# A two-layer decoder on one core: how split query and key rows pass through memory to be stacked, and where GpSimd adds two output biases

## Chip, cores and metric

The kernel runs on one core of a Trainium2 chip. The metric is the device time of one execution, in microseconds. The engines are named as in the profile: PE (TensorE), PEld (its weight loads), DVE (VectorE), ACT (ScalarE), POOL (GpSimd) and SP (SyncE, which here only issues DMAs).

## The reference, cut to what matters

Six sublayers over x of 8 sequences (b) of 256 rows and 256 columns, each followed by a layer norm. The change lies in the fourth (D) and fifth (E).

```python
def _L1_attn_ref(x, Wqkv, bqkv, Wout, bout, proj):      # stage D
    ...
    q, k, v = jnp.split(x @ Wqkv.T + bqkv, 3, axis=-1)  # 16 heads of 16, relu(q proj), relu(k proj), causal, chunks of 128
    ...
    return out @ Wout.T + bout
def _L1_xattn_ref(query, key_value, Wq, bq, Wk, bk, Wv, bv, Wo, bo):   # stage E
    ...
    q = (query @ Wq + bq).reshape(B, Nq, H, D).transpose(0, 2, 1, 3)
    k = (key_value @ Wk + bk).reshape(B, Nkv, H, D).transpose(0, 2, 1, 3)
    v = (key_value @ Wv + bv).reshape(B, Nkv, H, D).transpose(0, 2, 1, 3)
    attn = jnp.clip(jnp.einsum('bhqd,bhkd->bhqk', q, k) * scale, -CLAMP, CLAMP)
    attn = jax.nn.softmax(attn, axis=-1)
    ...
    x = jnp.einsum('bhqk,bhkd->bqhd', attn, v).reshape(B, Nq, Cq)
    return x @ Wo + bo
...
x = _layernorm(x + _L0_attn_ref(x, ...))        # A
x = _layernorm(x + _L0_xattn_ref(x, ctx_768, ...))   # B
x = _layernorm(x + _L0_ffn_ref(x, ...))         # C
x = _layernorm(x + _L1_attn_ref(x, ...))        # D
x = _layernorm(x + _L1_xattn_ref(x, ctx_768, ...))   # E
x = _layernorm(x + _L1_ffn_ref(x, ...))         # F, two of eight experts a token
```

In E a score is a product of a query and a key row of 16 numbers. The kernel keeps near fp32 accuracy with pairs: hi is the rounded value, lo is the rest.

## The kernel before

The stages A, B and C are done first. D and E run together as a software pipeline over the 8 sequences; then come F (experts, in blocks of tokens) and the last norm. The order inside D and E is written out by `de_steps` (L104): each item has a round in which it starts, a priority, and rounds for its steps. `in_rounds` sorts them, and every engine walks through the same list `DE` and does its own part of each step. Sequence b's E scores (`PAIR`, eight steps of two head pairs) start 18 rounds behind its D steps, so that they stand between D's steps of b+2.

What the change touches:

- `EPRE` steps 1 and 2 make keys and queries of E. PE multiplies, ACT writes `qk_hi` and `qk_raw` (L1362, L1365), POOL subtracts for `qk_lo` (L620). There is one `qk_hi` and one `qk_lo`: ACT and POOL wait until the tensor before (keys, then queries, `n = 2 * b + which`) is in memory (`w_qk`, L1360 and L619).
- `stack_heads` (L779) is SP's part. It stores hi and lo (128 rows each, L786) to the DRAM tensor `split_qk`, waits until both have landed (L787), and loads them back with their rows reordered: 8 loads of 16 partitions by 8 KB for each tensor (L795). Keys go into `k_e` (named `xt_lo` in the profile, since they lie in its room), queries into `q_e` (`xt_hi`). The matmul of scores (L1090) then contracts over 64 partitions that hold r = 0..3, one side stacked as hi, lo, hi, lo and the other as hi, hi, lo, lo. It waits for all 16 loads of b (L1084).
- SP issues the DMAs one by one. Its queue also carries the context load (L801) and the store of x rows (L806).
- `finish` on POOL (L583) adds the output bias to x in its step 0 (L592: two adds of 128x256 for b), for D in `DFIN` step 0 and for E in `EFIN` step 0, and takes the layer norm's power in step 1. The bias waits until PE has transposed the old x (`old.filled`, L589). DVE's `resid` (L1682) waits for it through `s_xb` (L1679).
- `EFIN` step 7 issues four indirect DMAs on POOL that scatter 128 codes of 4 bytes each into `slot_codes` (L640). `EFIN` step 7 of b-1 and step 0 of b share a round in the list, and step 7 stands first.

```python
load(held[part], f(src[:, :, :]).rearrange("p c s -> p (c s)"), w_qk)          # L786, once for hi, once for lo
...
heads = held[r // 2 if which else r % 2].rearrange("(i d j) s -> i d (j s)", i=2, d=DH)
...
load(f((q_e if which else k_e)[b % 2][rows, :, :]).rearrange("p j s -> p (j s)"), heads[i], l_qk[b % 2])   # L795
```

## Time and profile before

| what | value |
|---|---|
| three runs | 1616.68, 1610.22, 1615.24 us; median 1615.24 |
| the profiled execution's own time, and its span | 1623.73 us; 1621.9 us |
| mean granted TensorE clock in it | 0.904 |
| PE, PEld, DVE, ACT, POOL busy, share of the span | 83, 70, 68, 35, 50% |
| stretch 780 to 1210 us (most of D and E): PE, DVE, ACT, POOL busy | 338.8, 285.0, 164.1, 145.8 of 430 us |
| stretch 1210 to 1290 us (end of E, routing): the same | 38.4, 38.3, 16.4, 33.3 of 80 us |
| chain that ended last: share of DMA, of SP's queue | 10%, 2% |

Read it so: busy shares are averages over stages with different limits; for a change in D and E, what counts is the stretch from about 760 to 1290 us, and in it the waits of the engine that the others follow. A row of a timeline gives start, busy time, engine, line, operation, tiles and count, and in brackets how long the engine stood idle before it and who ended that.

### The profile page before, as it was taken

How to read it: one execution, taken by the hardware profiler on the slowest of the kernel's cores; microseconds unless marked ns; L12 is line 12 of the kernel's file. 1: busy time of each engine (PE TensorE's matmuls, PEld its weight loads, DVE VectorE, ACT ScalarE, POOL GpSimd, SP SyncE). 2: the span in 40 equal slices, each digit the busy share in tenths (PEclk: the TensorE clock that was granted, in tenths of full speed). 3: DMA queues.
4: the chain of work that ended last, by engine and by line, in shares of the span. 5: the costliest groups of instructions: out<-in, count | busy, mean ns of one | idle time of the engine just before them, and what ended most of it. 6: DMA issues, size and time to landing. Idle time of an engine off the chain costs nothing.

```text
span 1621.9 us, 23438 instructions
## 1 busy us (share of the span) xinstructions
PE 1347.4 (83%) x9047; PEld 1137.9 (70%) x9047; DVE 1109.1 (68%) x1877; ACT 561.0 (35%) x1138; POOL 816.9 (50%) x762
## 2 busy tenths in 40 slices
PE   5787799989989989978788989788656199999990
PEld 5776678868868878865566656556544199999990
DVE  5889776676576676634476767567654388888886
ACT  2355311111021121113244434334322166666662
POOL 3333556656566656640123334244335378888852
PEclk9896799999999999989899999899776599999995
DMA  5100233323223322210444155153340366666624
GB/s 164 30 16 11 69 92 91 104 85 92 77 91 91 104 78 79 84 59 7 78 83 78 38 67 71 26 84 57 59 59 7 110 239 230 219 212 236 219 72 156
DMA packets 53534, 154.99 MB, mean 96 GB/s; under 512 B 10822, under 2 KB 25641, under 8 KB 45488
## 3 DMA queue, kind: packets, MB, share of 16 engines
q1 hardware_dynamic: 41248, 91.87, 24.0%
q0 software_dynamic: 12176, 61.63, 10.8%
q8 instruction: 72, 1.18, 0.3%
q14 instruction: 38, 0.31, 0.1%
HBM read 136.60 MB, written 18.70 MB: 96 GB/s over the span
## 4 chain that ended last, share of the span: by engine, by line
PE 54%; DVE 19%; DMA 10%; issue 6%; ACT 5%; POOL 4%; SPq 2%; ACTq 0%; DVEq 0%; POOLq 0%
PE bank L385 12%; PE bank L387 12%; PE bank L386 12%; PE bank L1193 8%; DMA xt_hi<-split_qk 5%; PE bank L393 4%; DMA split_qk<-qk_lo 3%; PE bank L1035 2%; DVE hid_hi L1598 2%; SPq L706 2%; DVE topE L1723 2%; DVE hf L1614 1%; DVE shiftE L1732 1%; PE bank L1111 1%; PE bank L1022 1%
## 5 line engine op out<-in xcount | busy, mean ns | idle before, releaser
L512 POOL TENSOR_TENSOR wpiece_lo<-wraw,wpiece_hi 128x1024 fp32r<-128x1024 f32 x88 | 216.8, 2463 | 7.4
L1600 DVE TENSOR_TENSOR hid_lo<-hf,hid_hi 128x512 fp32r<-128x512 f32 x96 | 215.8, 2248 | 3.3
L385 PE MATMUL bank<-hid_hi,wpiece_lo 128*128 128x512 f32 x512 | 204.1, 399 | 13.3 <-DVE hid_lo L1600 13.3
L387 PE MATMUL bank<-hid_hi,wpiece_hi 128*128 128x512 f32 x512 | 202.6, 396 | 0.0
L386 PE MATMUL bank<-hid_lo,wpiece_hi 128*128 128x512 f32 x512 | 202.3, 395 | 0.0
L510 POOL TENSOR_SCALAR wpiece_hi<-wraw 128x1024 fp32r<-128x1024 f32 x88 | 95.6, 1086 | 192.6 <-PE bank L387 188.7
L1598 DVE CAST hid_hi<-hf 128x512 fp32r<-128x512 f32 x96 | 76.9, 801 | 131.1 <-ACT hf L1292 130.0
L626 POOL TENSOR_SCALAR staging<-staging 128x1024 f32<-128x1024 f32 x64 | 66.6, 1041 | 176.4 <-ACT staging L1377 176.3
L1292 ACT ACTIVATE hf<-bank,ffn_scales 128x512 f32<-128x512 f32 x64 | 44.1, 690 | 299.1 <-PE bank L387 299.1
L385 PEld LDWEIGHTS bank<-hid_hi,wpiece_lo 128*128 128x128 f32 x512 | 98.1, 192 | 39.2 <-DVE hid_lo L1600 19.0
L1723 DVE TENSOR_REDUCE topE<-bank 128x4 f32<-128x1024 f32 x64 | 77.9, 1218 | 65.8 <-PE bank L1090 65.7
L1377 ACT ACTIVATE staging<-bank 128x512 f32<-128x512 f32 x128 | 70.2, 596 | 151.3 <-PE bank L1111 86.4
L387 PEld LDWEIGHTS bank<-hid_hi,wpiece_hi 128*128 128x128 f32 x512 | 97.8, 191 | 20.8
L386 PEld LDWEIGHTS bank<-hid_lo,wpiece_hi 128*128 128x128 f32 x512 | 98.2, 192 | 20.3
L1193 PE MATMUL bank<-w_hi,gh_lo 128*128 128x256 f32 x368 | 105.8, 288 | 5.6 <-issue 2.6
L1434 ACT ACTIVATE gf<-bank,w1raw 128x256 f32<-128x256 f32 x184 | 77.2, 471 | 91.4 <-PE bank L387 91.4
L385 PE MATMUL bank<-xgT_hi,w_lo 128*128 128x256 f32 x368 | 106.7, 290 | 1.4 <-DVE xgT_lo L1850 1.4
L386 PE MATMUL bank<-xgT_lo,w_hi 128*128 128x256 f32 x368 | 104.6, 284 | 0.0
L387 PE MATMUL bank<-xgT_hi,w_hi 128*128 128x256 f32 x368 | 104.6, 284 | 0.0
L1193 PE MATMUL bank<-w_hi,gh_hi 128*128 128x256 f32 x368 | 104.1, 283 | 0.0
L1193 PE MATMUL bank<-w_lo,gh_hi 128*128 128x256 f32 x368 | 104.1, 283 | 0.0
L670 POOL TENSOR_TENSOR w_lo<-w2raw,w_hi 128x256 fp32r<-128x256 f32 x92 | 91.7, 1023 | 11.4 <-ACT w_hi L1409 10.9
(353 smaller groups left out, 3805.0 us busy)
## 6 DMA issues: line engine op xcount, KB each, us to landing
wraw<-in_C_w SPq DMA_DIRECT2D x88, 512.0 KB, 3.6
xt_lo<-split_qk SPq DMA_DIRECT2D x64, 128.0 KB, 5.2
xt_hi<-split_qk SPq DMA_DIRECT2D x64, 128.0 KB, 6.2
split_qk<-qk_hi SPq DMA_DIRECT2D x16, 256.0 KB, 4.4
split_qk<-qk_lo SPq DMA_DIRECT2D x16, 256.0 KB, 3.8
yc<-y_rows SPq DMA_DIRECT2D x16, 256.0 KB, 5.8
ctx_raw<-in_ctxT SPq DMA_DIRECT2D x16, 192.0 KB, 3.6
xraw<-in_xT SPq DMA_DIRECT2D x8, 256.0 KB, 3.8
```

What stands on the lines that cost most here:

```text
L385: pe.e.matmul(o, sl, mh, start=start and i == 0, stop=False)
L386: pe.e.matmul(o, sh, ml, start=False, stop=False)
L387: made = pe.e.matmul(o, sh, mh, start=False, stop=stop and i == n - 1)
L510: pool.mark(pool.e.tensor_scalar(pair[0], raw, 1.0, 0.0, ALU.mult, ALU.add))
L512: pool.e.tensor_tensor(pair[1], raw, f(pair[0]), ALU.subtract).then_inc(done, 1)
L670: pool.e.tensor_tensor(w2[n % 6][1][:, 1, :], w2_cols(*divmod(n, NQ))[:, 1, :], f(w2[n % 6][0][:, 1, :]), ALU.subtract).then_inc(s_w2lp, 1)
L1193: made = pe.e.matmul(u.ap[:, t * D:(t + 1) * D], hh[:, i, st], ww[:, i, :], start=fc == 0 and k == 0 and t == 0, stop=fc == FC - 1 and k == 2,
L1377: act.e.activation(prob_e[n % 3][:, i, :, :], u.ap[:, :].rearrange("p (k s) -> p k s", k=TT), ACT.Exp, scale=scale_e).then_inc(u.drained, 1)
L1434: made = act.e.activation(gf[n % 2][:, i * BT:(i + 1) * BT], u.ap[:, i * BT:(i + 1) * BT], ACT.Gelu, bias=w1raw[j % 4][:, c:c + 1])
L1598: dve.mark(dve.e.tensor_copy(hi[:, o, :], hf[o % 2][:, :]))
L1600: dve.e.tensor_tensor(lo[:, o, :], hf[o % 2][:, :], f(hi[:, o, :]), ALU.subtract).then_inc(s_hid, 1)
L1723: dve.mark(dve.e.tensor_reduce(top[:, :], scores, AX.X, ALU.max))
```

## The change

The stores now put the rows where they will be read. `split_qk` is laid out as two tensors of [2 (i), 4 (r), 64 rows, 512]. Of hi and of lo each, SP issues four stores of 64 partitions by 2 KB (i = 0, 1 for two values of r), so each value is written twice. One load of 128 partitions by 8 KB then brings a tensor back. `w_qk` becomes one semaphore for keys and one for queries. POOL adds D's bias in step `XT` (behind the transposes of C's x) and E's bias in `DFIN` step 3 (behind the transposes of D's x).

```diff
@@ -241,7 +241,7 @@
 
         x_rows = nc.dram_tensor("x_rows", (B * S, D), F32, kind="Internal").ap()
         y_rows = nc.dram_tensor("y_rows", (TOPK * B * S, D), F32, kind="Internal").ap()
-        split_qk = ring(2, lambda i: nc.dram_tensor(f"split_qk{i}", (2, 2, P, KC * S), F32, kind="Internal").ap())
+        split_qk = ring(2, lambda i: nc.dram_tensor(f"split_qk{i}", (2, 2, 4, 4 * DH, KC * S), F32, kind="Internal").ap())
         slot_codes = nc.dram_tensor("slot_codes", (NE * B * S + BT, 1), U32, kind="Internal").ap()
 
         def xt(b):
@@ -345,7 +345,7 @@
         s_dwo, s_ew = sem("dwo"), sem("ew")
         s_xb, s_cthi = {k: sem(f"xb_{k}") for k in "DE"}, {k: sem(f"ct_hi_{k}") for k in "DE"}
         s_vone, s_prob = sem("ones"), sem("e_prob")
-        s_qkhi, s_qklo, w_qk, l_qk = sem("e_qkhi"), sem("e_qklo"), sem("w_qk"), ring(2, lambda i: sem(f"l_qk{i}"))
+        s_qkhi, s_qklo, w_qk, l_qk = sem("e_qkhi"), sem("e_qklo"), ring(2, lambda i: sem(f"w_qk{i}")), ring(2, lambda i: sem(f"l_qk{i}"))
         s_rm, s_re, s_rf, s_rb, s_rs, s_sh = (sem(f"r_{n}") for n in ("m", "e", "f", "b", "s", "sh"))
         s_seen, s_slot = sem("r_seen"), sem("r_slot")
         w_rows, w_codes = ring(2, lambda i: sem(f"w_rows{i}")), ring(2, lambda i: sem(f"w_codes{i}"))
@@ -463,6 +463,11 @@
             u = use[stage, "x", b]
             line.wait_ge(u.drained, u.done)
 
+        def stored(line, n):
+
+            for which in range(2):
+                line.wait_ge(w_qk[which], 16 * 8 * ((n + 1 - which) // 2))
+
         def piece_done(m):
 
             s, n = divmod(m, NPIECE)
@@ -580,19 +585,17 @@
             for b in range(B - BPS, B):
                 ln_pow(pool, "C", b)
 
-            def finish(stage, step, b, bo, l_bo, n_bo):
-                if step == 0:
-                    before_it = "C" if stage == "D" else "D"
-                    old = use[before_it, "x", b]
-                    pool.wait_ge(l_bo, n_bo)
-                    pool.wait_ge(s_x[before_it], b + 1)
-                    pool.wait_ge(old.filled, old.full)
-                    for t in range(TT):
-                        x = x_tok[:, b * TT + t, :]
-                        made = pool.e.tensor_tensor(x, x, bo[:, :], ALU.add)
-                    made.then_inc(s_xb[stage], 1)
-                elif step == 1:
-                    ln_pow(pool, stage, b)
+            def add_bias(stage, b, bo, l_bo, n_bo):
+
+                before_it = "C" if stage == "D" else "D"
+                old = use[before_it, "x", b]
+                pool.wait_ge(l_bo, n_bo)
+                pool.wait_ge(s_x[before_it], b + 1)
+                pool.wait_ge(old.filled, old.full)
+                for t in range(TT):
+                    x = x_tok[:, b * TT + t, :]
+                    made = pool.e.tensor_tensor(x, x, bo[:, :], ALU.add)
+                made.then_inc(s_xb[stage], 1)
 
             last = use["C", "y", B - 1]
             pool.wait_ge(last.drained, last.done)
@@ -608,15 +611,19 @@
                     for i, n, pair, src in ((1, 48, eq, "E_wq"), (1, 64, ek, "E_wk"), (0, 80, ev, "E_wv"), (1, 80, eo, "E_wo")):
                         pool.wait_ge(l_stage[i], n)
                         split([w[:, :, :] for w in pair], staged(i, a[src]), s_ew)
-                elif name == "DFIN":
-                    finish("D", step, *args, dbo, l_db, 80)
+                elif name == "XT":
+                    add_bias("D", *args, dbo, l_db, 80)
+                elif name == "DFIN" and step == 1:
+                    ln_pow(pool, "D", *args)
+                elif name == "DFIN" and step == 3:
+                    add_bias("E", *args, ebo, l_eb, 64)
                 elif name == "EPRE" and step == 0:
                     context(B + args[0])
                 elif name == "EPRE" and step < 3:
                     b, = args
                     n, u = 2 * b + step - 1, use["E", "kq"[step - 1], b]
                     pool.wait_ge(u.drained, u.done)
-                    pool.wait_ge(w_qk, 32 * n)
+                    stored(pool, n)
                     pool.e.tensor_tensor(qk_lo[:, :, :], qk_raw[:, :, :], f(qk_hi[:, :, :]), ALU.subtract).then_inc(s_qklo, 1)
                 elif name == "PAIR" and step == 1:
                     b, p = args
@@ -626,8 +633,9 @@
                     pool.e.tensor_scalar(pr, pr, 1.0, 0.0, ALU.min, ALU.max).then_inc(s_prob, 1)
                 elif name == "EFIN":
                     b, = args
-                    finish("E", step, b, ebo, l_eb, 64)
-                    if step == 6 and b < B - 1:
+                    if step == 1:
+                        ln_pow(pool, "E", b)
+                    elif step == 6 and b < B - 1:
                         one_hot(pool, b)
                         set_shares(pool, b)
                     elif step == 7:
@@ -780,19 +788,19 @@
 
 
                 n, held = 2 * b + which, split_qk[b % 2][which]
-                sp.wait_ge(l_qk[b % 2], 16 * 16 * (b // 2))
+                sp.wait_ge(l_qk[b % 2], 16 * 2 * (b // 2))
                 for part, (src, done) in enumerate(((qk_hi, s_qkhi), (qk_lo, s_qklo))):
                     sp.wait_ge(done, n + 1)
-                    load(held[part], f(src[:, :, :]).rearrange("p c s -> p (c s)"), w_qk)
-                sp.wait_ge(w_qk, 32 * (n + 1))
+                    for r in range(4):
+                        if (r // 2 if which else r % 2) == part:
+                            for i in range(2):
+                                load(held[i, r], f(src[i * 4 * DH:(i + 1) * 4 * DH, :, :]).rearrange("p c s -> p (c s)"), w_qk[which])
+                sp.wait_ge(w_qk[which], 16 * 8 * (b + 1))
                 if b >= 2:
                     old = use["E", "s", b - 2, PAIRS - 1]
                     sp.wait_ge(old.filled, old.full)
-                for r in range(4):
-                    heads = held[r // 2 if which else r % 2].rearrange("(i d j) s -> i d (j s)", i=2, d=DH)
-                    for i in range(2):
-                        rows = slice((4 * i + r) * DH, (4 * i + r + 1) * DH)
-                        load(f((q_e if which else k_e)[b % 2][rows, :, :]).rearrange("p j s -> p (j s)"), heads[i], l_qk[b % 2])
+                load(f((q_e if which else k_e)[b % 2]).rearrange("p j s -> p (j s)"),
+                     held.rearrange("i r (d j) s -> (i r d) (j s)", j=4), l_qk[b % 2])
 
             for name, step, args in DE:
                 b = args[0]
@@ -1081,7 +1089,7 @@
                 elif name == "PAIR" and step == 0:
                     b, p = args
                     u = use["E", "s", b, p]
-                    pe.wait_ge(l_qk[b % 2], 16 * 16 * (b // 2 + 1))
+                    pe.wait_ge(l_qk[b % 2], 16 * 2 * (b // 2 + 1))
                     pe.wait_ge(u.drained, u.turn)
                     for t in range(TT):
                         for i in range(2):
@@ -1357,7 +1365,7 @@
                     act.wait_ge(l_eb, 64)
                     act.wait_ge(u.filled, u.full)
                     act.wait_ge(s_qklo, n)
-                    act.wait_ge(w_qk, 32 * n)
+                    stored(act, n)
                     for c in range(KC):
                         made = act.e.activation(qk_hi[:, c, :], u.ap[:, c * S:(c + 1) * S], ACT.Identity, bias=bias[:, c:c + 1])
                     made.then_inc(s_qkhi, 1)

```

**SP, keys and then queries of one sequence** (`xt_lo` are the keys stacked, `xt_hi` the queries). Before:

```order
L706 DMA split_qk<-qk_hi 128x512 [waits e_qkhi]
L706 DMA split_qk<-qk_lo 128x512 [waits e_qklo]
L706 DMA xt_lo<-split_qk 16x2048 [waits w_qk]
L706 DMA xt_lo<-split_qk 16x2048 x7
L706 DMA split_qk<-qk_hi 128x512 [waits e_qkhi]
L706 DMA split_qk<-qk_lo 128x512 [waits e_qklo]
L706 DMA xt_hi<-split_qk 16x2048 [waits w_qk]
L706 DMA xt_hi<-split_qk 16x2048 x7
```

Now, in the same place:

```order
L714 DMA split_qk<-qk_hi 64x512 [waits e_qkhi]
L714 DMA split_qk<-qk_hi 64x512 x3
L714 DMA split_qk<-qk_lo 64x512 [waits e_qklo]
L714 DMA split_qk<-qk_lo 64x512 x3
L714 DMA xt_lo<-split_qk 128x2048 [waits w_qk0]
L714 DMA split_qk<-qk_hi 64x512 [waits e_qkhi]
L714 DMA split_qk<-qk_hi 64x512 x3
L714 DMA split_qk<-qk_lo 64x512 [waits e_qklo]
L714 DMA split_qk<-qk_lo 64x512 x3
L714 DMA xt_hi<-split_qk 128x2048 [waits w_qk1]
```

Twenty DMAs a sequence become eighteen: the loads fall from 16 to 2, the stores rise from 4 to 16.

**POOL, in the middle of D and E, from one sequence's scatter on** (`ebo` is E's bias, `dbo` D's). Before:

```order
L640 DMA slot_codes<-codes,slot0 16640x1 [waits r_slot]
L640 DMA slot_codes<-codes,slot0 16640x1 x3
L592 TENSOR_TENSOR x_tok<-x_tok,ebo 128x256 [waits lnD_x]
L592 TENSOR_TENSOR x_tok<-x_tok,ebo 128x256
L626 TENSOR_SCALAR staging<-staging 128x1024 [waits drained4]
L419 TENSOR_TENSOR lnE_rstd1<-lnE_rstd1,minus_half 128x2 [waits lnE_var]
```

Now, the same place, and then the place ahead of the keys' lo part of the next sequence:

```order
L648 DMA slot_codes<-codes,slot0 16640x1 [waits r_slot]
L648 DMA slot_codes<-codes,slot0 16640x1 x3
L633 TENSOR_SCALAR staging<-staging 128x1024 [waits drained4]
L419 TENSOR_TENSOR lnE_rstd1<-lnE_rstd1,minus_half 128x2 [waits lnE_var]
```

```order
L597 TENSOR_TENSOR x_tok<-x_tok,dbo 128x256 [waits filled4,lnC_x]
L597 TENSOR_TENSOR x_tok<-x_tok,dbo 128x256
L633 TENSOR_SCALAR staging<-staging 128x1024 [waits drained6]
L597 TENSOR_TENSOR x_tok<-x_tok,ebo 128x256 [waits filled4,lnD_x]
L597 TENSOR_TENSOR x_tok<-x_tok,ebo 128x256
L627 TENSOR_TENSOR qk_lo<-qk_raw,qk_hi 128x512 [waits w_qk1,drained5]
```

E's bias no longer stands behind the four scatters of the sequence before it; both biases now stand ahead of a `qk_lo` of keys. PE, DVE and ACT keep their instructions in their order.

## Rows read from the trace of the kernel before

**Rows 1.** PE's waits, 700 to 1240 us: total us, times, longest

```profile
PE bank L1090 <- DMA xt_hi<-split_qk: 62.1, 7, 17.9
PE bank L1035 <- DVE shiftE L1732: 21.6, 17, 2.0
```

**Rows 2.** Timeline of PE: the first scores of b = 0, 1, 3, 4, 5, 6, 7

```profile
793.98 0.80 PE L1090 MATMUL bank<-xt_lo,xt_hi 64*128 64x256 f32 x4 [6.72 <-DMA xt_hi<-split_qk]
841.39 0.50 PE L1090 MATMUL bank<-xt_lo,xt_hi 64*128 64x256 f32 x4 [2.17 <-DMA xt_hi<-split_qk]
957.93 0.80 PE L1090 MATMUL bank<-xt_lo,xt_hi 64*128 64x256 f32 x4 [6.78 <-DMA xt_hi<-split_qk]
1023.40 0.80 PE L1090 MATMUL bank<-xt_lo,xt_hi 64*128 64x256 f32 x4 [9.98 <-DMA xt_hi<-split_qk]
1084.84 0.80 PE L1090 MATMUL bank<-xt_lo,xt_hi 64*128 64x256 f32 x4 [6.29 <-DMA xt_hi<-split_qk]
1146.18 0.80 PE L1090 MATMUL bank<-xt_lo,xt_hi 64*128 64x256 f32 x4 [12.24 <-DMA xt_hi<-split_qk]
1200.37 0.79 PE L1090 MATMUL bank<-xt_lo,xt_hi 64*128 64x256 f32 x4 [17.89 <-DMA xt_hi<-split_qk]
```

**Rows 3.** The chain: start, us until landed, lo stores (one of keys, seven of queries)

```profile
771.05 2.02 DMA split_qk<-qk_lo
777.18 6.96 DMA split_qk<-qk_lo
...
826.03 5.00 DMA split_qk<-qk_lo
...
935.28 5.34 DMA split_qk<-qk_lo
...
997.48 5.08 DMA split_qk<-qk_lo
...
1062.61 5.07 DMA split_qk<-qk_lo
...
1123.61 7.91 DMA split_qk<-qk_lo
...
1176.04 12.04 DMA split_qk<-qk_lo
```

**Rows 4.** The chain: the last of eight query loads, b = 0 and b = 4

```profile
787.29 6.64 DMA xt_hi<-split_qk
...
1005.71 17.64 DMA xt_hi<-split_qk
```

**Rows 5.** Timeline of POOL: the first scatter beside the loads of b = 4, 6, 7

```profile
1002.03 1.11 POOL L640 DMA_INDIRECT slot_codes<-codes,slot  x1 [0.17 <-issue]
...
1125.73 1.11 POOL L640 DMA_INDIRECT slot_codes<-codes,slot  x1 [0.54 <-DVE slot L1788]
...
1177.96 1.11 POOL L640 DMA_INDIRECT slot_codes<-codes,slot  x1 [0.41 <-DVE slot L1788]
```

**Rows 6.** Stretches: length, busy us of PE, PEld, DVE, ACT, POOL, then PEclk, DMA share, GB/s

```profile
993.00:1000.00 7.00, 7.00 (x64) 5.34 (x62) 4.48 (x16) 4.04 (x10) 3.11 (x8) 1.00 1.02 133
...
1006.00:1016.00 10.00, 7.42 (x66) 5.28 (x62) 7.18 (x17) 3.35 (x6) 5.15 (x6) 1.00 0.89 52
1285.50:1289.00 3.50, 0.40 (x2) 0.28 (x2) 1.16 (x6) 0.00 (x0) 1.56 (x2) 0.50 0.87 295
```

**Rows 7.** Timeline of PE, right behind the wait of b = 3

```profile
958.66 1.97 PE L393 MATMUL bank<-ident,shiftE 128*128 128x128 f32 x8
```

**Rows 8.** Timeline of DVE: `resid` of E for b = 6 and b = 7

```profile
1230.33 0.69 DVE L1682 TENSOR_TENSOR resid<-bank,x_tok 128x512 f32<-128x512 f32 x1 [3.50 <-POOL x_tok L592]
...
1256.84 0.69 DVE L1682 TENSOR_TENSOR resid<-bank,x_tok 128x512 f32<-128x512 f32 x1 [5.08 <-POOL x_tok L592]
```

**Rows 9.** Timeline of PE: the last product that the `resid` of b = 7 reads

```profile
1254.33 0.41 PE L387 MATMUL bank<-eo_hi,ctxT_E_hi 128*128 128x256 f32 x1
```

**Rows 10.** One line of DVE: ns min/median/max, first and last start

```profile
L1726 DVE SCALAR_TENSOR_TENSOR topE<-topE,lowE x64: 161/164/1253, 796.1 to 1233.5; 128x4 f32<-128x4 f32 x64
```

## The prediction, made before the changed kernel had run

> **What bounds the kernel now.** The page's chain of waits puts 10% of the span on DMAs, most of it on the stacked query and key rows. So I read next who waits for them: the waits of TensorE over stages D and E. PE stands idle 62.1 us for `xt_hi`, the last loads of the stacked queries, and the next wait there, for DVE's `shiftE`, is 21.6 us over 17 times [rows 1]. The timeline shows the 62.1 us one by one: 6.72, 2.17, 6.78, 9.98, 6.29, 12.24 and 17.89 us ahead of the first scores of b = 0, 1, 3, 4, 5, 6 and 7 [rows 2]; b = 2 does not wait. PE is the engine that the others follow there (338.8 of 430 us busy in the table), so those waits are on the path.
>
> Then the chain, for what a wait is made of. The lo part of the queries is ready and its store issued at 777.18, 826.03, 935.28, 997.48, 1062.61, 1123.61 and 1176.04 [rows 3]. From there to PE's first scores [rows 2] it takes 16.8, 15.4, 22.7, 25.9, 22.2, 22.6 and 24.3 us. For b = 4 that is 5.1 us for the store to land, 3.1 us until the last of eight loads is issued at 1005.71, and 17.6 us until it lands [rows 3, 4]. For b = 0 the last load lands in 6.6 us [rows 4]. The difference is the scatter: for b = 4 POOL's four scatters begin at 1002.03 [rows 5], and from 1006 to 1016 52 GB/s move where the keys' loads alone moved 133 GB/s at a full DMA share [rows 6]. A 128-row load of 8 KB rows (an expert's weights) runs at 295 GB/s [rows 6].
>
> **The change, part by part.**
>
> *The load.* 1 MB at 133 GB/s is 7.9 us, and b = 0 shows 3.1 + 6.6 = 9.7 us from the first issue to landing [rows 4]. At 295 GB/s it is 3.6 us, and landing adds about the 2.0 us that an unhindered store takes from issue to landing [rows 3]: 5.6 us. I take 5.6, since the row at 295 GB/s has the new load's shape; the upper bound is 9.7 (no gain).
> The Trainium skill (SBUF — State Buffer, "Door 1: The DMA port swizzle") says that 16 partitions reach 4 of 16 ports, 104 GB/s at 1 MiB, and 128 partitions 328 GB/s. The trace agrees in kind: 133 against 295 GB/s [rows 6].
>
> *The stores.* Hi and lo are now four stores each. SP issues at 0.46 us apiece (the last of eight loads starts 3.1 us behind the first), so the last lo store is issued 1.4 us behind the first and lands 2.0 us later [rows 3]: 3.4 us. Twice the bytes leave from 64 partitions; no row has that shape. Lower bound 3.4; upper bound, 512 KB at the 16-row rate of 133 GB/s behind as much of hi, about 8 us. I take 4.0, near the row of the unhindered store.
> By the same table of the skill, 64 partitions reach 8 ports and 196 GB/s, so 512 KB would take 2.7 us and a sequence's path would be about 1 us longer than my sum has it, some 6 us less gain in all; no row here shows it.
>
> *Path of a query, new.* 4.0 + 5.6 = 9.6 us from the ready lo part to the scores, where nothing else runs.
> - b = 0: ACT's queries wait for the keys' stores, which land about 2 us later than now, and the queries' stores meet the keys' load (1.5 us). 16.8 - 9.6 - 3.5 = 3.7 us saved of 6.7.
> - b = 1: 15.4 - 9.6 = 5.8, more than the 2.2 us waited. Saved 2.2.
> - b = 3, 4, 5: the scatters start some 4.6 us behind the lo store (997.48 and 1002.03 for b = 4 [rows 3, 5]), just as the load goes out. At 52 GB/s for 10 us [rows 6] they can cost a load anything from 0 to 11.0 us, the difference between b = 4 and b = 0 [rows 4]; I take 6, between the ends, since half of the new load is through before the queues are full. Saved: 22.7, 25.9, 22.2 less 9.6 less 6 = 7.1, 10.3, 6.6, each just over the 6.8, 10.0 and 6.3 waited. Saved 23.1.
> - b = 6, 7: the scatters start 2.1 and 1.9 us behind the lo store [rows 3, 5] and hit stores and load; I take 8. b = 7 also has its keys' stores late (2 us; its own lo store took 12.0 us [rows 3]). Saved 22.6 - 17.6 = 5.0 of 12.2 and 24.3 - 19.6 = 4.7 of 17.9.
>
> Sum: 38.7 us of 62.1.
>
> *The clock.* Behind a long wait the four score matmuls take 0.80 us, behind a short one 0.50 [rows 2], and the next eight transposes 1.97 us [rows 7]. Twice the time is the lower of the clock's two levels (a granted clock of 0.50, as in the third stretch of [rows 6], is 1.2 for 2.4 GHz), and PE had stood idle before it. Where a wait goes, I estimate 1 to 2 us saved behind it, bounds 0 and 2.5. Three waits go whole and others in part: 5 us.
>
> *E's bias.* For b = 6 `resid` waits 3.50 us for POOL, which issues four scatters first; PE and DVE are nearly empty there, and this stands on the path. For b = 7 the last product ends at 1254.74 [rows 9] and `resid` starts at 1256.84 [rows 8]: 2.1 of its 5.08 us of idleness. Moved, the adds come 18 rounds of the list early. Saved 5.6 us. Two more such waits, at b = 4 and 5, lie beside PE's waits for loads; they count for nothing alone, but would have come up next.
>
> *D's bias* moves along on an engine that is busy 146 of 430 us there; zero. Both biases now stand ahead of a keys' `qk_lo`. Their cover is POOL's idleness, and if it were gone the keys, not the queries, would be some 3 us later. SP's queue gets shorter (18 issues for 20), and the context load and the store of x rows behind it come earlier; zero.
>
> *What is late next.* With PE's pauses gone, the norm's chain and `shiftE` have less time beside them: 3 us lost, bounds 0 and 15 [rows 1].
>
> Together 38.7 + 5 + 5.6 - 3 = 46 us. The profiled execution took 1623.7 us, so it would become 1577.7. The median of the runs shown is 1615.2, 8.5 below it, so the median becomes **1569**.
>
> **The rivals.**
> 1. *The scatter holds the loads all the same.* The full 11.0 us come on top for b = 3 to 7. For: 52 GB/s whatever the ports [rows 6]. Against: one load has fewer pieces left when the scatters start. Saved: 3.7 + 2.2 for b = 0 and 1, 2.1, 5.3, 1.6, 2.0 and 1.7 for the rest, and the tail's 5.6: 24.2 us, 1591 us. Chance 0.17.
> 2. *All waits go.* 62.1, 7 of clock, 5.6: 75 us, 1540 us. It needs stores and load to overtake the scatters. Against: 12.0 us for one store of b = 7 [rows 3]. Chance 0.10.
> 3. *DVE and POOL collide.* The moved adds hold DVE: `L1726` takes 164 ns at the median and 1253 at most [rows 10], so one collision can cost 1.1 us. Sixteen pairs of adds in new places: 16 us, 1585 us. They could collide in their old places too, so the sign is open. Chance 0.05. The Trainium skill (SBUF — State Buffer, "Who interferes with whom") says that a DVE operation with two SBUF inputs waits for a whole GpSimd operation that reads SBUF, as `L1726` has.
> 4. *The waits move, nothing is won.* The chain of the norm and `shiftE` takes the place of the loads. Against: b = 2 has no wait for a load, and nothing long in its place. 1612 us, chance 0.04.
> 5. *Slower: the stores are the new wait.* Eight stores of 64 rows run at the 16-row rate: 1 MB a tensor is 7.9 us, for keys and again for queries, ahead of a load that stays at 9.7 us (the ports are not what limits it). Then each of seven paths grows by about 5 us: 35 us, less the tail's 5.6: 1645 us. It decides from where the stores cost more than the load gives back, a lo part that lands over 8 us after it is ready with a load at 9.7. Chance 0.04.
>
> **How the numbers follow.** The forecast has 0.60, the rivals 0.17, 0.10, 0.05, 0.04 and 0.04. The range is 1541 to 1595: below, all waits gone; above, the scatter in full, with 4 us for stores that land late. That leaves out rivals 4 and 5 and edges, under 2 in 10. 0.5% is 8 us, about what a measurement of this kernel can tell from no change. Faster by more: forecast and rivals 1 to 3, 0.92; within: rival 4, 0.04; slower: rival 5, 0.04.
>
> **What would show it.** In the changed profile: PE's wait for `xt_hi` near 23 us, almost all of it at b = 6 and 7; one query load landing in about 6 us at b = 0 to 2 and 6 to 16 us beside scatters; lo stores landing about 4 us after the first issue; no wait of `resid` for POOL; behind b = 4 no scores at 0.80 us. The prediction is wrong if b = 3 to 5 still wait over 3 us each (rival 1), if DVE or the norm's chain shows new waits of PE over 15 us in total (rival 4), or if a load of 128 rows takes over 8 us where no scatter runs.

## The result, and the profile after

The changed kernel takes 1573.1 us at the median (1571.1 to 1576.0) where the kernel before takes 1616.0 (1610.2 to 1624.4). The ratio is 0.973 with an interval of 0.969 to 0.978: faster. The prediction was 1569, its range 1541 to 1595.

The profiled execution of the changed kernel has a span of 1569.7 us and takes 1571.6, against 1621.9 and 1623.7 before: 52.1 us less. From the page of the changed kernel, busy time by engine, memory traffic, and the chain by engine:

```profile
PE 1332.3 (85%) x9047; PEld 1128.4 (72%) x9047; DVE 1114.2 (71%) x1877; ACT 559.8 (36%) x1138; POOL 816.0 (52%) x762
...
HBM read 136.60 MB, written 27.08 MB: 104 GB/s over the span
...
PE 58%; DVE 23%; issue 6%; ACT 5%; DMA 5%; SPq 2%; POOL 2%; ACTq 0%; DVEq 0%; POOLq 0%
```

DMAs are now 5% of the chain where they were 10%, although 8.4 MB more are written (27.1 for 18.7 MB).

To see where the 52.1 us went, cut both executions at the first product that makes a `feat` of D (`qkD` by `proj`) and at the start of the last scatter: stages A to C, then D and E. The windows of the changed kernel (length, busy us of PE, PEld, DVE, ACT, POOL, then PEclk, DMA share, GB/s):

```profile
0.00:711.20 711.20, 629.65 (x3182) 536.73 (x3182) 490.49 (x682) 162.71 (x310) 378.56 (x276) 0.94 0.27 80
711.20:1221.80 510.60, 418.95 (x3565) 312.66 (x3565) 348.73 (x685) 200.54 (x420) 189.82 (x246) 0.90 0.27 75
```

The same windows of the kernel before:

```profile
0.00:717.80 717.80, 636.75 (x3180) 542.55 (x3180) 489.32 (x682) 162.81 (x310) 381.38 (x278) 0.93 0.26 79
717.80:1274.60 556.80, 428.16 (x3565) 317.52 (x3565) 344.76 (x685) 201.78 (x420) 187.15 (x244) 0.86 0.34 54
```

D and E became 46.2 us shorter (556.8 to 510.6). In them PE is busy for 9.2 us less (428.2 to 419.0) with the same 3565 matmuls, at a mean granted clock of 0.90 for 0.86, and idle for 36.9 us less (128.6 to 91.7). Stages A to C, which the change doesn't touch, ran 6.6 us shorter in this execution, again nearly all of it PE's busy time (7.1 us). That part belongs to the execution, not to the change, and something of the kind can be in D and E too: two more profiles of the changed kernel, shown further on, have 516.1 and 518.5 us there, with PE busy for 424.5 and 423.8. The medians differ by 42.9 us.

PE's waits over stages D and E (700 to 1200 us, the total, the times and the longest), which answer to [rows 1]:

```profile
PE bank L1043 <- DVE shiftE L1740: 25.1, 22, 2.0
PE bank L1098 <- DMA xt_hi<-split_qk: 20.8, 3, 10.2
```

The wait for the query loads fell from 62.1 to 20.8 us, and the norm's `shiftE` is now the larger of the two, 3.5 us up (0.8 up in the second profile of this kernel). Which three waits are left, in the timeline of PE (as [rows 2]; the idle time stands in brackets):

```profile
782.65 0.51 PE L1098 MATMUL bank<-xt_lo,xt_hi 64*128 64x256 f32 x4 [1.63 <-DMA xt_hi<-split_qk]
1103.47 0.80 PE L1098 MATMUL bank<-xt_lo,xt_hi 64*128 64x256 f32 x4 [10.19 <-DMA xt_hi<-split_qk]
1153.61 0.80 PE L1098 MATMUL bank<-xt_lo,xt_hi 64*128 64x256 f32 x4 [8.99 <-DMA xt_hi<-split_qk]
```

These are b = 0, 6 and 7. Sequences 1 to 5 don't wait any more. The chain has the pieces of the same three (as [rows 3, 4]; start and us until landed, and of the four lo stores the last one's):

```profile
773.57 4.18 DMA split_qk<-qk_lo
777.76 4.84 DMA xt_hi<-split_qk
...
1087.46 8.28 DMA split_qk<-qk_lo
1095.75 7.67 DMA xt_hi<-split_qk
...
1137.43 8.34 DMA split_qk<-qk_lo
1145.79 7.78 DMA xt_hi<-split_qk
```

What is 4.2 and 4.8 us at b = 0 is 8.3 and 7.7 beside scatters. The order of events for b = 4 and b = 6 shows why one waits and the other doesn't. SP's timeline at b = 4, where four stores of lo precede one load:

```profile
976.70 2.54 SPq L714 DMA_DIRECT2D split_qk<-qk_lo  x4
981.50 0.33 SPq L714 DMA_DIRECT2D xt_hi<-split_qk  x1
```

and POOL's first scatter beside the loads of b = 3, 4 and 6 (each is followed by three more, 1.3 us apart):

```profile
925.57 1.24 POOL L648 DMA_INDIRECT slot_codes<-codes,slot  x1 [0.62 <-issue]
...
981.05 1.11 POOL L648 DMA_INDIRECT slot_codes<-codes,slot  x1 [0.17 <-issue]
...
1087.89 1.11 POOL L648 DMA_INDIRECT slot_codes<-codes,slot  x1 [0.17 <-issue]
```

For b = 4 the stores had landed and the load went out 0.45 us behind the start of the first scatter's issue; it still landed in 4.8 us. For b = 6 the scatters came 2.4 us behind the first lo store's issue, and neither the stores nor the load behind them landed in time:

```profile
1085.52 2.54 SPq L714 DMA_DIRECT2D split_qk<-qk_lo  x4
1095.75 0.33 SPq L714 DMA_DIRECT2D xt_hi<-split_qk  x1
```

Query loads take 4.8, 5.0, 4.9, 4.8, 4.8, 8.6, 7.7 and 7.8 us for b = 0 to 7. From the first lo store's issue to the load's issue it is 6.1, 4.9, 4.8, 4.4, 4.8, 4.8, 10.2 and 10.3 us. In the stretch of b = 0's load 305 GB/s move. The stretch of b = 6's stores, 1088 to 1098 us, has a mean of 58, but that is no steady rate (the last two lines):

```profile
778.50:782.60 4.10, 2.52 (x16) 1.39 (x14) 1.88 (x6) 1.02 (x1) 0.00 (x0) 1.00 0.84 305
1087.50:1089.90 2.40, 2.40 (x30) 1.86 (x29) 2.33 (x4) 1.39 (x3) 1.91 (x3) 1.00 0.84 285
1090.50:1095.70 5.20, 2.78 (x32) 1.69 (x28) 5.06 (x8) 1.36 (x3) 4.66 (x5) 1.00 0.02 1
```

The stores' bytes go at 285 GB/s and are through by about 1090. Then next to nothing moves for over 5 us, at a DMA share of 0.02, and the last store counts as landed only at 1095.74. What the scatters put off here is the landing, not the moving of bytes. The loads beside scatters look different. This is the load of b = 5, then that of b = 6:

```profile
1037.50:1043.20 5.70, 4.79 (x52) 4.04 (x50) 4.24 (x7) 0.38 (x1) 3.81 (x4) 1.00 0.86 53
1095.90:1100.50 4.60, 0.00 (x0) 0.00 (x0) 1.96 (x5) 1.09 (x2) 0.00 (x0) 0.71 0.72 50
```

For some 5 us they move 50 to 53 GB/s at a high DMA share, as in [rows 6], and then the rest at 273 and 349 GB/s (1043.2 to 1046 and 1100.5 to 1103.4 us). Why the one and why the other, the trace does not show.

DVE's `resid` of E, which waited 3.50 and 5.08 us for POOL [rows 8], now waits for PE's own product:

```profile
1181.16 0.69 DVE L1690 TENSOR_TENSOR resid<-bank,x_tok 128x512 f32<-128x512 f32 x1 [0.44 <-PE bank L387]
1204.00 0.69 DVE L1690 TENSOR_TENSOR resid<-bank,x_tok 128x512 f32<-128x512 f32 x1 [3.02 <-PE bank L387]
```

One wait is new, and the prediction had it for b = 0 and b = 7 alone: ACT, about to write the queries' `qk_hi`, stands for the keys' stores at all eight sequences. ACT's waits of the changed kernel:

```profile
ACT qk_hi L1370 <- DMA split_qk<-qk_lo: 34.1, 8, 5.3
```

It was 4.5 us over two times before.

### The profile page after: what moved, and what is told of

The parts are those of the page before. It is cut to its first block, busy times and chain, and to the rows that moved or that the text cites. A ratio compares the mean times of both kernels' runs of the same rounds, so it can differ in the third digit from the quotient of the medians.

```text
span 1569.7 us, 23427 instructions
## 1 busy us (share of the span) xinstructions
PE 1332.3 (85%) x9047; PEld 1128.4 (72%) x9047; DVE 1114.2 (71%) x1877; ACT 559.8 (36%) x1138; POOL 816.0 (52%) x762
## 3 DMA queue, kind: packets, MB, share of 16 engines
q1 hardware_dynamic: 45088, 100.26, 21.6%
## 4 chain that ended last, share of the span: by engine, by line
PE 58%; DVE 23%; issue 6%; ACT 5%; DMA 5%; SPq 2%; POOL 2%; ACTq 0%; DVEq 0%; POOLq 0%
PE bank L385 13%; PE bank L387 13%; PE bank L386 13%; PE bank L1201 8%; PE bank L393 4%; DVE topE L1731 2%; DVE shiftE L1740 2%; DMA split_qk<-qk_lo 2%; SPq L714 2%; PE bank L1043 2%; DVE hid_hi L1606 2%; DVE hf L1622 2%; DMA xt_hi<-split_qk 1%; PE bank L1119 1%; PE bank L1030 1%
## 5 line engine op out<-in xcount | busy, mean ns | idle before, releaser
L385 PE MATMUL bank<-hid_hi,wpiece_lo 128*128 128x512 f32 x512 | 202.6, 396 | 12.2 <-DVE hid_lo L1608 12.2
L387 PEld LDWEIGHTS bank<-hid_hi,wpiece_hi 128*128 128x128 f32 x512 | 97.1, 190 | 20.5
L1442 ACT ACTIVATE gf<-bank,w1raw 128x256 f32<-128x256 f32 x184 | 77.2, 471 | 91.7 <-PE bank L387 91.7
L1201 PE MATMUL bank<-w_hi,gh_lo 128*128 128x256 f32 x368 | 106.0, 288 | 4.3 <-issue 1.6
L1201 PE MATMUL bank<-w_hi,gh_hi 128*128 128x256 f32 x368 | 104.2, 283 | 0.0
L1201 PE MATMUL bank<-w_lo,gh_hi 128*128 128x256 f32 x368 | 104.1, 283 | 0.0
L678 POOL TENSOR_TENSOR w_lo<-w2raw,w_hi 128x256 fp32r<-128x256 f32 x92 | 90.7, 1013 | 13.0 <-ACT w_hi L1417 12.4
```

What stands on the lines that cost most here:

```text
L385: pe.e.matmul(o, sl, mh, start=start and i == 0, stop=False)
L387: made = pe.e.matmul(o, sh, mh, start=False, stop=stop and i == n - 1)
L678: pool.e.tensor_tensor(w2[n % 6][1][:, 1, :], w2_cols(*divmod(n, NQ))[:, 1, :], f(w2[n % 6][0][:, 1, :]), ALU.subtract).then_inc(s_w2lp, 1)
L1201: made = pe.e.matmul(u.ap[:, t * D:(t + 1) * D], hh[:, i, st], ww[:, i, :], start=fc == 0 and k == 0 and t == 0, stop=fc == FC - 1 and k == 2,
L1442: made = act.e.activation(gf[n % 2][:, i * BT:(i + 1) * BT], u.ap[:, i * BT:(i + 1) * BT], ACT.Gelu, bias=w1raw[j % 4][:, c:c + 1])
```

## The experiments

They ran as three jobs on different chips. The kernel before took 1628.3, 1615.1 and 1633.9 us at the median there. The chips of the first and third job also took some 16 to 20 us longer over the experts' stage, which no kernel here touches (280 us from the first to the last of the experts' products, L1201, in the two executions above, 296 to 301 there). So kernels are compared within a job, by ratios to the kernel before, and by the length of stages D and E in their profiles, cut as above.

### First job: the parts

**The stacking alone.** The changed kernel, with both biases added where they were.

```diff
-                elif name == "XT":
+                elif name == "DFIN" and step == 0:
...
-                elif name == "DFIN" and step == 3:
-                    add_bias("E", *args, ebo, l_eb, 64)
...
+                    if step == 0:
+                        add_bias("E", b, ebo, l_eb, 64)
```

> The changed kernel with both output biases added in their old places (DFIN and EFIN step 0). Theory: most of the 43 us comes from the stacking; what the bias move gives is the tail (5.6 us) and the two waits of resid behind the scatters at b = 4 and 5, which are no longer hidden beside waits for loads: 1579 to 1584 us, DVE's resid waits for POOL 12 to 20 us in total. Rival (the bias move carries much of the gain): over 1592 us.

Measured: 1606.4 us, ratio 0.985 (0.978 to 0.991). PE waits 20.4 us for the query loads, as in the changed kernel. D and E take 514.8 us, 4.2 more than there. What came back is the wait of `resid` (DVE's waits):

```profile
DVE resid L1690 <- POOL x_tok L597: 16.3, 4, 5.1
```

So the stacking alone takes PE's wait down. DVE waits for POOL as expected. The time lies in the range of the rival (over 1592), not of the theory (1579 to 1584), but on a chip where the kernel before is 12 us slower too; its ratio makes 1591 us of the first 1616.0, between the two. What the bias adds is not told by medians from two jobs; the third job takes it up again.

**The biases alone.** The kernel before, with both biases behind the transposes.

```diff
-                elif name == "DFIN":
-                    finish("D", step, *args, dbo, l_db, 80)
+                elif name == "XT":
+                    finish("D", 0, *args, dbo, l_db, 80)
+                elif name == "DFIN" and step == 1:
+                    finish("D", 1, *args, dbo, l_db, 80)
+                elif name == "DFIN" and step == 3:
+                    finish("E", 0, *args, ebo, l_eb, 64)
...
-                    finish("E", step, b, ebo, l_eb, 64)
-                    if step == 6 and b < B - 1:
+                    if step == 1:
+                        finish("E", 1, b, ebo, l_eb, 64)
+                    elif step == 6 and b < B - 1:
```

> The kernel before with the biases in their new places. Theory: only the tail shortens, about 5.6 us: 1610 us, PE's wait for xt_hi stays near 62 us (up to 5 us more, where the wait for resid had stood beside it), no wait of resid for POOL. Rival (the bias move carries much of the gain): under 1600 us.

Measured: 1628.1 us, ratio 0.999 (0.993 to 1.005). `resid` has no wait for POOL. PE's wait for the query loads is 61.9 us over 7 times, with 14.9 the longest, against 62.1 and 17.9 [rows 1]. D and E are 8.6 us shorter in the profiled execution, which the median doesn't bear out. The 5.6 us that the theory expected at the tail lie within the interval, so they are neither shown nor excluded. Without the stacking the moved biases show no gain in the times; nothing in this kernel shows a loss from them either.

**The old shape of loads behind the new stores.** The changed kernel with eight loads of 16 partitions by 8 KB for each tensor (the counts that SP and PE wait for follow, here and in the next run; left out).

```diff
-                load(f((q_e if which else k_e)[b % 2]).rearrange("p j s -> p (j s)"),
-                     held.rearrange("i r (d j) s -> (i r d) (j s)", j=4), l_qk[b % 2])
+                rows_of = held.rearrange("i r (d j) s -> (i r d) (j s)", j=4)
+                for g in range(8):
+                    load(f((q_e if which else k_e)[b % 2][g * DH:(g + 1) * DH, :, :]).rearrange("p j s -> p (j s)"),
+                         rows_of[g * DH:(g + 1) * DH, :], l_qk[b % 2])
```

> The changed kernel, but each tensor is loaded by eight DMAs of 16 partitions x 8 KB again; stores as changed. Theory (the partitions that a load reaches set its time): the keys' loads move about 133 GB/s again, a query's loads land 9 to 10 us after the first issue and 15 us or more beside scatters; PE's wait for xt_hi is 45 to 75 us and the time 1600 to 1620 us. Rival A (the number of DMAs sets it): the same as the next run. Rival B (neither, the gain is elsewhere): within 5 us of 1573.

Measured: 1678.0 us, ratio 1.030 (1.023 to 1.036), slower than the kernel before. PE waits 100.9 us over 8 times, D and E take 596.4 us, and SP's queue is 24% of the chain from 760 to 1260 us. The chain at b = 0 and the lo stores of b = 3:

```profile
784.57 4.81 DMA split_qk<-qk_lo
792.83 6.19 DMA xt_hi<-split_qk
...
955.63 13.28 DMA split_qk<-qk_lo
```

At b = 0 it takes 14.4 us from 784.57 until the last load has landed (792.83 + 6.19), where the changed kernel takes 9.0 (773.57 to 782.60). The later b are hit harder. The keys' eight loads hold SP for 3.6 us, so that the queries' stores go out later, into the scatters, and the lo stores of b = 3 take 13.3 us. Both expectations were too low. The outcome is that of rival 5 of the prediction, stores that cost more with a load that gives nothing back, but not by its mechanism, a slow rate of the stores themselves: at b = 0 to 2 it is 6.8, 6.3 and 7.1 us from the first lo store's issue to the load's, and 12.8 to 20.5 from b = 3 on, where the scatters are. In the changed kernel it is 4.8 at b = 4, against 5.1 before, so there the stores cost nothing more.

**Eight loads of all 128 partitions.** The same number of loads as in the run above, each over 128 partitions with 1 KB a partition.

```diff
-                load(f((q_e if which else k_e)[b % 2]).rearrange("p j s -> p (j s)"),
-                     held.rearrange("i r (d j) s -> (i r d) (j s)", j=4), l_qk[b % 2])
+                rows_of = held.rearrange("i r (d j) s -> (i r d) (j s)", j=4)
+                for g in range(8):
+                    load(f((q_e if which else k_e)[b % 2][:, g, :]), rows_of[:, g * S:(g + 1) * S], l_qk[b % 2])
```

> The changed kernel, but each tensor is loaded by eight DMAs of 128 partitions x 1 KB (the same bytes, eight issues). Theory (the partitions that a load reaches set its time): the last of eight is issued 3 to 4.5 us after the first and lands 2.4 us behind that, about the 5 to 6 us of one load; 1573 to 1580 us, PE's wait for xt_hi 20 to 30 us. Rival A (the number of DMAs sets it): 1600 us or more, as the eight loads of 16 partitions.

Measured: 1638.2 us, ratio 1.006 (1.000 to 1.012). PE waits 68.0 us over 7 times, D and E take 560.6 us. At b = 0 the last load lands in 3.8 us (6.2 in the run above). But SP spends 4.6 us on issuing the keys' loads, and at b = 3 that pushes the queries' lo stores to within 1.2 us of the scatters (SP's timeline, then POOL's, then the chain):

```profile
928.40 4.55 SPq L714 DMA_DIRECT2D xt_lo<-split_qk  x8
933.00 2.38 SPq L714 DMA_DIRECT2D split_qk<-qk_hi  x4
935.42 2.52 SPq L714 DMA_DIRECT2D split_qk<-qk_lo  x4
```

```profile
936.60 1.24 POOL L648 DMA_INDIRECT slot_codes<-codes,slot  x1 [0.62 <-issue]
```

```profile
937.34 9.90 DMA split_qk<-qk_lo
950.48 7.87 DMA xt_hi<-split_qk
```

The theory had 1573 to 1580 us and a wait of 20 to 30, the rival 1600 us or more. So the theory, that the partitions that a load reaches make the whole difference, falls; nor do eight loads cost the same whatever their shape, as the rival has it. The table has the three kernels that share the new stores:

| loads of a tensor | issues | partitions each | D and E, us | PE's wait for query loads, us |
|---|---|---|---|---|
| 8 x 16 partitions | 8 | 16 | 596.4 | 100.9 |
| 8 x 128 partitions, 1 KB | 8 | 128 | 560.6 | 68.0 |
| 1 x 128 partitions, 8 KB (the change) | 1 | 128 | 510.6 | 20.8 |

All 128 partitions give 35.8 us. One issue in place of eight gives 50.0 us (42.1 and 44.5 with the other two profiles of the changed kernel), part of it SP's time and part of it what that time lets the scatters catch; 8 KB instead of 1 KB of a partition at once is in the second step too, and was not tried apart. (The third row's profile is from another chip than the first two; the stretch of D and E differs by 4 to 8 us between the changed kernel's three profiles: 510.6, 516.1, 518.5.)

### Second job: the scatters and the hidden wait

**The changed kernel again**, as the measure for this job.

> The changed kernel once more, beside the runs of this call. Theory and rival alike: 0.973 of the kernel before, within 0.005; PE's wait for xt_hi about 21 us, at b = 0, 6 and 7.

Measured: 1581.7 us, ratio 0.980 (0.972 to 0.988), a little outside the 0.968 to 0.978 expected, with an interval that overlaps it; D and E 516.1 us, PE's wait 22.8 us over 3 times. At b = 6 the first scatter starts 2.4 us behind the first lo store's issue (1095.38 and 1092.97), as in the first profile. Yet the last lo store takes 5.7 us and the load 10.9, where it had been 8.3 and 7.7. The split between the two varies, the sum hardly: 16.6 and 16.0.

What this second profile changes is the reading of b = 4. Its load went out 0.59 us behind the start of the first scatter, hardly later than in the first profile, and took 8.3 us where it had been 4.8. PE did not wait for it. Its bytes were through by about 994, as with the stores above, and the landing came at 997.8:

```profile
990.50:994.20 3.70, 2.80 (x33) 2.19 (x34) 3.39 (x5) 0.38 (x1) 3.06 (x4) 1.00 0.74 268
994.30:997.70 3.40, 3.40 (x32) 2.96 (x34) 2.20 (x5) 0.00 (x0) 0.58 (x1) 1.00 0.01 0
```

The loads that went out close behind the first scatter, in this kernel's first two profiles and in that of the stacking alone:

| profile, b | load issued behind the first scatter, us | landed in, us |
|---|---|---|
| first, 3 | 0.17 | 4.8 |
| second, 3 | 0.38 | 4.8 |
| first, 4 | 0.45 | 4.8 |
| second, 4 | 0.59 | 8.3 |
| first, 5 | 1.47 | 8.6 |
| second, 5 | 1.65 | 8.5 |
| stacking alone, 4 | 1.98 | 12.4 |

In these seven the landing goes by the head start over the scatters, and b = 4 stands at the edge: between 0.45 and 0.59 us it changed sides.

**The scatters three rounds later.**

```diff
-        items.append((e + 13, 5, "EFIN", (b,), (0, 1, 2, 4, 4, 5, 7, 8)))
+        items.append((e + 13, 5, "EFIN", (b,), (0, 1, 2, 4, 4, 5, 7, 8, 11)))
...
-                    elif step == 7:
-                        if b < B - 1:
-                            add_seen(pool, b)
+                    elif step == 7 and b < B - 1:
+                        add_seen(pool, b)
+                    elif step == 8:
```

> The changed kernel with the four scatters of a sequence issued three rounds later (a step 8 of EFIN), behind the query load of the sequence then being stacked. Theory (what is left of PE's wait at b = 6 and 7 is the scatter beside stores and load): without it a path is 4.8 + 4.9 us, so that PE would wait 1.9 and 0.6 us there instead of 10.2 and 9.0; PE's wait for xt_hi falls from 21 to 3 to 6 us, and the time to about 0.963 of the kernel before. Rival (SP's queue and the keys' stores make those waits): the wait stays over 15 us and the ratio at 0.973.

Measured: 1565.1 us, ratio 0.969 (0.961 to 0.978). This is PE's wait for the query loads:

```profile
PE bank L1098 <- DMA xt_hi<-split_qk: 6.4, 3, 2.4
```

It was expected at 3 to 6 us, and the ratio at 0.963. D and E take 500.1 us, 16.0 less than in the measure, and this is the chain at b = 7:

```profile
1131.82 4.89 DMA split_qk<-qk_lo
1136.72 4.83 DMA xt_hi<-split_qk
```

The two make 9.7 us, for 15.9 in the measure. So the scatters are what is left of PE's wait in the changed kernel, and it is an order in time that decides: for b = 7 the first of them now starts at 1145.63, when the load has landed. The medians of this run and the measure are 16.6 us apart, and its slowest execution (1574.3) is faster than the fastest of the measure (1579.1).

**The same edit on the kernel before.**

> The kernel before with the scatters three rounds later and nothing else. Theory (the scatter made about 7 to 10 us of each path from b = 3 on): PE's wait for xt_hi falls from 62 to about 25 us (6.7 and 2.2 at b = 0 and 1, some 5 and 10 at b = 6 and 7), resid no longer waits behind scatters, and the ratio is 0.972 to 0.980, nearly what the whole change gives. Rival (the 16-row loads are the wait, scatter or not): PE's wait stays over 45 us, ratio over 0.985.

Measured: 1584.8 us, ratio 0.981 (0.972 to 0.990), within 3.1 us of the changed kernel's 1581.7 in the same job. PE's wait fell from 62.1 us [rows 1] to this, and D and E take 516.0 us:

```profile
PE bank L1090 <- DMA xt_hi<-split_qk: 27.7, 4, 11.8
```

The theory's 25 us and 0.972 to 0.980 were nearly met, and the rival, that the 16-row loads are the wait whatever the scatters do, falls. One number in a list of rounds does as much as the change, as far as these executions (four of each, spread over 11 to 21 us) can tell. Together they give 50.0 us (1615.1 to 1565.1) where each alone gives 33.4 and 30.3, 63.7 in all. So they overlap by some 14 us, on medians that are uncertain by about as much; PE's waits say the same, 39.3 and 34.4 us less alone and 55.7 together. That fits the places: PE's four waits that are left here are at b = 0, 1, 6 and 7, so either edit takes away the waits of b = 3 to 5, 23.1 us in [rows 2].

**A second `qk_lo`.** The late scatters, and in addition two buffers for the lo part and separate semaphores for hi and lo, so that ACT waits for the keys' hi stores alone (the tile of ones moves to make room; left out).

```diff
-        qk_raw, qk_hi, qk_lo = sbp("qk_raw", [P, KC, S]), sbp("qk_hi", [P, KC, S], F32R), sbp("qk_lo", [P, KC, S], F32R)
+        qk_raw, qk_hi, qk_lo = sbp("qk_raw", [P, KC, S]), sbp("qk_hi", [P, KC, S], F32R), ring(2, lambda i: sbp(f"qk_lo{i}", [P, KC, S], F32R))
...
-                line.wait_ge(w_qk[which], 16 * 8 * ((n + 1 - which) // 2))
+                line.wait_ge(w_qk[2 * which], 16 * 4 * ((n + 1 - which) // 2))
```

> The changed kernel with late scatters and with a second buffer for qk_lo, so that ACT's queries wait for the keys' hi stores alone (the tile of ones goes to the room of stages A and B to make space). Theory: ACT's 34 us of waiting for the keys' stores fall under 12 us, PE's wait for xt_hi to under 3 us, and the ratio to 0.958 to 0.963. Rival (the keys' stores were hidden): ACT waits less, but the time is that of the run with late scatters alone, within 0.003.

Measured: 1566.8 us, ratio 0.972 (0.963 to 0.980), the same as with late scatters alone. ACT's wait for stores went from 36.1 us over 8 times to 2.0 over one, as meant, and no gain came of it: the rival holds. PE's wait for the query loads rose from 6.4 to 16.4 us in the profile, and D and E take 505.2 us, 5.1 more. At b = 6 the queries' hi stores go out 0.4 us behind the keys' load and run beside it:

```profile
1087.52 0.33 SPq L718 DMA_DIRECT2D xt_lo<-split_qk  x1
1087.89 2.37 SPq L718 DMA_DIRECT2D split_qk<-qk_hi  x4
1090.66 2.40 SPq L718 DMA_DIRECT2D split_qk<-qk_lo  x4
1097.51 0.33 SPq L718 DMA_DIRECT2D xt_hi<-split_qk  x1
```

From the lo stores' first issue to the query load it is 6.9 us there, against 5.2 with one buffer (1088.56 to 1093.76). So taking ACT's wait away lengthened the path behind it, and the two can have cancelled: that the 34 us of the changed kernel cost nothing is not shown, only that this way of removing them gains nothing. Whether a later place in the list would let the second buffer gain was not tried.

### Third job: the biases on top of the stacking

**The changed kernel and the stacking alone**, side by side, in five rounds.

> The changed kernel once more, as the measure for the run beside it, on one chip and in five rounds. All theories: 0.973 to 0.980 of the kernel before, TensorE waiting 20 to 24 us for the query loads in stages D and E.

> The changed kernel with the two output biases back in their old places, beside the changed kernel on one chip. My theory (the moved bias of E takes one wait off the tail, 4 to 6 us, and the stores and loads do the rest): 4 to 6 us above the changed kernel, ratio to the kernel before 0.976 to 0.984. Rival (the biases are worth nothing once the stacking is done, what lies between the two earlier runs was the chip): within 2 us of the changed kernel. Second rival (the biases are worth 15 us or more, since the waits of resid for POOL at four sequences, 16.3 us in the earlier profile, come back in full): 12 us or more above.

Measured: 1600.0 us, ratio 0.978 (0.973 to 0.982), for the changed kernel, and 1611.5, ratio 0.986 (0.982 to 0.990), with the biases in their old places. The medians are 11.5 us apart, but single executions of either spread over 15 to 17 us, and the two profiled ones differ by only 2.0 us over D and E (518.5 and 520.5). In these two PE is busy 4.5 us longer in the changed kernel (423.8 and 419.3) with the same matmuls, which hides part of a difference. Where the bias costs is seen at the end. DVE's timeline, first the stacking alone:

```profile
1189.08 0.69 DVE L1690 TENSOR_TENSOR resid<-bank,x_tok 128x512 f32<-128x512 f32 x1 [3.52 <-POOL x_tok L597]
...
1215.59 0.69 DVE L1690 TENSOR_TENSOR resid<-bank,x_tok 128x512 f32<-128x512 f32 x1 [5.08 <-POOL x_tok L597]
```

and the changed kernel:

```profile
1193.76 0.69 DVE L1690 TENSOR_TENSOR resid<-bank,x_tok 128x512 f32<-128x512 f32 x1 [0.43 <-PE bank L387]
...
1216.63 0.69 DVE L1690 TENSOR_TENSOR resid<-bank,x_tok 128x512 f32<-128x512 f32 x1 [3.02 <-PE bank L387]
```

At b = 6 the wait is 3.1 us shorter, and from there to `resid` of b = 7 it takes 22.9 us in place of 26.5: 3.6 us. Together 6.7 us at the tail. The median's 11.5 lies between my 4 to 6 and the second rival's 12 or more; from the spread of six executions each, I estimate the difference at 11 us with an uncertainty of 8 either way. That the biases are worth nothing once the stacking is done (within 2 us) is not borne out. How much more than the tail's 6.7 us they give stays open.

## Why the prediction was right

**The bound** was read rightly. The wait of PE for the query loads is what gave way, 62.1 to 20.8 us, against a forecast of 23.

**The path of a query** was to be 9.6 us where nothing else runs: 4.0 for stores and 5.6 for the load. At b = 2 and 4 it is 4.8 + 4.9 and 4.8 + 4.8: 9.7 and 9.6. The sum is right by luck, by two errors that cancel. The load is 0.8 us shorter than taken, moving 305 GB/s. The stores are 0.8 longer: SP takes 0.60 to 0.65 us for one of 64 rows, not the 0.45 of a 16-row load, so that the last goes out 1.9 us behind the first, not 1.4; and at b = 4 it lands 2.9 us behind its issue, not 2.0 (the keys' last one lands in 2.4). The Trainium skill (SBUF — State Buffer, "Door 1: The DMA port swizzle") would have had stores of 64 partitions cost a path 1 us more; they cost 0.8 more. The trace agrees with the 196 GB/s that it gives for them: from 1077.5 to 1081 us, where the keys' stores move alone, it shows 203 GB/s at a DMA share of 0.88. But a store of 128 KB every 0.65 us is 202 GB/s as well, so the trace doesn't tell the rate from the issue time.

**A row misread.** The 133 GB/s of [rows 6] are not the keys' loads alone, as the prediction has it: the queries' hi and lo stores were issued in that stretch too (995.19 and 997.48). From 1172.5 to 1175.5, where the keys' loads of b = 7 are alone, the kernel before moves 167 GB/s. The forecast took only upper bounds and rival 5 from this row.

**Sequence by sequence.** b = 0 was to keep 3.0 us of wait and keeps 1.6; b = 1 and b = 3 to 5 were to keep none, and keep none. b = 6 was to keep 7.2 (12.2 less 5.0) and keeps 10.2, b = 7 13.2 and keeps 9.0. Their paths from the first lo store to the landed load are 17.9 and 18.1 us, forecast 17.6 and 19.6. At b = 6 the path became 4.6 us shorter and the wait only 2.0: the sum took the one for the other, but PE came to these scores 2.6 us earlier, counted from the lo store, and so waited longer. The two errors, 3.0 up and 4.2 down, nearly cancel in the total.

**The step that failed within this** is the 6 us that the scatter was to cost at b = 3, 4 and 5. In the first profile it cost nothing at b = 3 and 4 (loads of 4.8 us) and 3.8 us at b = 5 (8.6 less 4.8); in the second 3.5 at b = 4, and in that of the stacking alone 7.6, where PE then waited 3.05 us. The price was taken from the slow rate of [rows 6], 52 GB/s for 10 us. A load that goes out 1.5 us behind the first scatter does meet such a rate, for 5.7 us; one that goes out up to 0.45 us behind it escapes, and what is held back in the stores of b = 6 is the landing. What its cost goes by is the head start over the first scatter, which the term left out. The outcome there was the same only because 6 us was just what could be lost without a wait.

**The clock** was sized at 5 us. In the first profile PE is busy 9.2 us less over D and E with the same matmuls, and the mean granted clock is 0.90 for 0.86. But the other two profiles of the changed kernel have only 3.7 and 4.4 less than the one profile of the kernel before (424.5 and 423.8 for 428.2, at 0.88 and 0.89), and stages A to C, which the change doesn't touch, differ by 7.1 in the first. So the direction is borne out, and a size between 4 and 9 us, which holds the forecast's 5 but does not confirm it. The places were right: at b = 6 and 7, where PE still stood idle before them, the first scores take 0.80 us, and the first ones of b = 3 to 5 take 0.50. Later scores of b = 4 and 5 at 0.79 us remain, so the sign "no scores at 0.80 us behind b = 4" did not come true.

**E's bias** was sized at 5.6 us. The tail shows 6.7, the profiles of D and E 2.0 (6.5 but for PE's longer busy time in one of them) and 4.2, the medians of the third job 11.5.

**What is late next** was sized at 3 us lost. `shiftE` is 3.5 us up (21.6 to 25.1), in the second profile of the changed kernel 0.8 (22.4).

**The sum** was 46 us and D and E became 46.2 us shorter. That it fits so closely is luck: by the other two profiles it is 40.7 and 38.3. In it PE's idle time fell by 36.9, not by the 41.3 that its wait for query loads alone fell, so other idle time grew by 4.4. The profiled execution's 52.1 us have 6.6 from stages A to C, so that they don't speak against the sum; the medians' 42.9 are 3 below it. The step from profile to median had two errors that cancel in part as well: the profiled execution took 1571.6 us and not 1577.7, and the median lies 1.4 above it and not 8.5 below. The chips of the second and third job gave 33.4 and 33.9 us between medians, ratios of 0.980 and 0.978. So 0.973 is the largest gain of three, and the term of 46 us was rather too high than too low over all of them.

**The rivals.** Rival 1 (the scatter holds all loads from b = 3 on) holds for b = 6 and 7, partly for b = 5, not for b = 3, and for b = 4 in one profile and not in the other; it was a matter of what lands before the scatters, and late scatters show what it is worth: 16 us. Rival 2 (all waits go) is nearly what happens with late scatters, at 1565.1 us for 1615.1 rather than 75 us less; PE then still idles 85.1 of 500.1 us. Rival 3, DVE and POOL in collision, shows in DVE's busy time, at under a third of its price: over D and E it is 348.7 and 348.9 us with the biases moved and 344.2 and 343.8 with the stacking alone, each time with the same 685 instructions. Some 5 us on an engine with room to spare, and in the third job the moved biases are faster all the same. Rival 4 would have needed a new wait of over 15 us. Rival 5's outcome, not its mechanism, was seen in the run with the old loads behind the new stores, 40 to 50 us slower than the kernel before by profile or median (596.4 for 556.8 over D and E; 1678.0 for 1628.3).

**What I did not see at all** is that moving the scatters alone was about as good as the change. The prediction had them as the difference between b = 4 and b = 0, and priced them as a term that limits the gain, without asking what it would be worth to move them.

## What to carry to other kernels

When a DMA is late, ask both how long it takes alone and what it meets: here the same 1 MB took 4.8 us alone and 7.7 to 10.9 behind scatters, and moving four small indirect DMAs by three rounds gave 30 us to the old loads and 17 to the new. Look where in a stretch the bytes move before you call its mean a rate: 58 GB/s over 10 us were 285 in the first two and 1 in five of the rest. Here the round trip was best with the fewest issues that still cover all partitions; the issuing queue's own time (0.5 to 0.65 us each) delays what stands behind it. A wait that appears on an engine off the path, such as ACT's 34 us, need not cost anything: the one way of taking it away that was tried gave nothing. And profile a kernel more than once before you explain 5 us of busy time by the change.
